# Scores of the middle attention: two products over 128 partitions in place of three over 64

## The chip, the core and the metric

The kernel runs on one core of a Trainium2 chip, as one launch. The metric is the device time of that core in microseconds (us). Engines are named as in the profile: PE is TensorE (matmuls, and transposes as matmuls), PEld its weight loads, DVE VectorE, ACT ScalarE, POOL GpSimd, SP SyncE.

## The reference

Two layers of a graph network over 625 nodes with 512 features. Each layer adds a graph part and a linear attention to x, and then a feed-forward part. What the change touches is the feed-forward part of the first layer, a full softmax attention whose weights a small router picks out of three sets:

```python
def gqa(x, wq, wk, wv, wo, n_kv):        # 8 heads of 64, x is the layer norm of 625 rows
    q = (x @ wq).reshape(B, S, N_HEADS, D_K).transpose(0, 2, 1, 3)
    k = (x @ wk).reshape(B, S, n_kv, D_K).transpose(0, 2, 1, 3)
    ...
    scores = jnp.einsum('bhqd,bhkd->bhqk', q, k) / jnp.sqrt(jnp.float32(D_K))
    attn = jax.nn.softmax(scores, axis=-1)
    out = jnp.einsum('bhqk,bhkd->bhqd', attn, v)
    out = out.transpose(0, 2, 1, 3).reshape(B, S, D_MODEL)
    return out @ wo
```

The second layer then has an edge part (20625 edges) and, as its feed-forward part, a product of the input with 128 matrices of 512x512, which takes the greater part of the kernel's time.

## The kernel before, in words

All engines run programs written out by hand, each in its own fixed order, and wait for each other by semaphores. The rows are tiled as 5 tiles of 125 nodes (T = 5, P = 125). Wide matmul operands are float32 values split in two: a rounded part ("h", written by ACT as it copies PSUM out) and the rest ("l", the value minus the rounded part, written by DVE). A product of two such operands is `product` (L1694 to L1700): h by h (L1698), h by l (L1699) and l by h (L1700), three matmuls into one PSUM group; l by l is left out.

PSUM is used as four slots of two banks. Work that fills a slot is a unit; `UNITS` lists all units in the order in which PE makes them, the slot is the unit's number modulo 4, and `begin` waits until the unit that had the slot last is drained.

The middle attention's units are, in order: `q1` (4 units: queries, transposed, two heads of 64 features on the 128 partitions of each), `k1` (4, keys likewise), `v1` (3, values by rows), then the list `ATTENTION`, then `proj1`.

- For each `q1` and `k1` unit PE runs 24 matmuls; ACT writes QFh or KFh (`upper`, L807) and DVE QFl or KFl (L1377). Between them ACT rounds the next weight matrix (L817), and POOL takes its rest (L687).
- An item is one tile of 125 queries of one head, 40 in all, five to a head. For an item PE makes `score` (two halves of 314 keys, each one `product` over the 64 partitions of the head's features); DVE takes the negated row maximum (negmax, L1388); ACT the exponential with its row sum (L967); DVE corrects the sum and inverts it (L1393, L1396); POOL scales the row (L732); PE turns it in five transposes (`probT`, L1920); ACT and DVE split the turned item (L978 and L807 for PTh, L1405 and L1124 for PTl).
- The order on PE is score of item i, then the transposes of item i-2. Once the five items of a head are turned, `attn` follows: 30 matmuls (PTh, PTl by VFh, VFl), whose result ACT and DVE split into XTh and XTl. Around it two items are taken together: score, score, attn, ten transposes.

The lines that matter are those of `score` on PE:

```python
u, r, o = ("score", item), item // T // 2, 64 * (item // T % 2)
begin(u)
if item == 0:
    wait_drained(pe, ("k1", K - 1))
...
ins = product(slot(u)[0:P, h, 0:HN], (QFh[o:o + 64, r, c], QFl[o:o + 64, r, c]),
              (KFh[o:o + 64, r, keys], KFl[o:o + 64, r, keys]), True, True)
```

Of the kernel before, what the change touches and what calls it, by code (L numbers as in the profile page):

```python
# [4 lines left out]
F32 = mybir.dt.float32  # L5
# [10 lines left out]
P = 125  # L16
T = N // P
K = D // 128
NT = 628
# [137 lines left out]
def splits(unit):  # L157

    return sum(u[0] in SPLIT for u in UNITS[:NUMBER[unit] + 1])
# [16 lines left out]
def halves(buf):  # L176

    return buf.rearrange("p (h n) -> p h n", h=2)


def build(nc, A, out):
    with ExitStack() as ctx:
        def sb(name, shape, dt, scope=ctx):
            return scope.enter_context(nc.sbuf_tensor(name, shape, dt))
# [3 lines left out]


        X = sb("X", [P, T, D], F32)  # L190
        XN = sb("XN", [P, T, D], F32)
        XTh = sb("XTh", [128, K, NT], F32R)
        XTl = sb("XTl", [128, K, NT], F32R)
# [100 lines left out]
            OTl = sb("OTl", [128, K, NT], F32R, s)  # L294

        with ExitStack() as s:
            QFh = sb("QFh", [128, K, NT], F32R, s)
            QFl = sb("QFl", [128, K, NT], F32R, s)
            KFh = sb("KFh", [128, K, NT], F32R, s)
            KFl = sb("KFl", [128, K, NT], F32R, s)  # L300
            VFh = sb("VFh", [P, T, D], F32R, s)
            VFl = sb("VFl", [P, T, D], F32R, s)
            PTh = sb("PTh", [P, T, NT], F32R, s)
            PTl = sb("PTl", [P, T, NT], F32R, s)
            prob = sb("prob", [P, 4, NT], F32, s)

        with ExitStack() as s:
            K2h = sb("K2h", [P, T, D], F32R, s)
# [165 lines left out]

        def slot(unit):
            return PS[:, 2 * SLOT[unit]:2 * SLOT[unit] + 2, :]

        def name_of(w):
            return WEIGHTS[w][0]
# [319 lines left out]
        def _(act):  # L799
# [6 lines left out]
            def upper(unit, dst, src, scale=1.0):  # L806
                a.activation(dst, src, ACT.Copy, scale=scale).then_inc(upper_ready, 1)  # L807

            def wait_filled(unit):
                act.wait_ge(filled, NUMBER[unit] + 1)  # L810
# [135 lines left out]
            transposed_upper("xt1")  # L946
            weight_upper(WEIGHT["F_q"])
            weight_upper(WEIGHT["F_k"])
            for stage, dst, scale in (("q1", QFh, DH ** -0.5), ("k1", KFh, 1.0)):
                for f in range(K):  # L950
                    u = (stage, f)
                    wait_filled(u)
                    upper(u, halves(dst[:, f]), slot(u)[:, :, 0:HN], scale)
                weight_upper(WEIGHT["F_v" if stage == "q1" else "F_o"])
            for m, tiles in enumerate(TILES):
                u = ("v1", m)
                wait_filled(u)
# [131 lines left out]
        def _(dve):  # L1089
# [280 lines left out]
            v.scalar_tensor_tensor(out=choice[0:1, 0:1], in0=choose[0:1, 1:2], scalar=2.0, in1=choose[0:1, 2:3],  # L1370
                                   op0=ALU.add, op1=ALU.mult).then_inc(chosen, 1)
            transposed_rest("xt1")
            for stage, up, dst, scale in (("q1", QFh, QFl, DH ** -0.5), ("k1", KFh, KFl, 1.0)):
                for f in range(K):
                    u = (stage, f)
                    dve.wait_ge(upper_ready, splits(u))
                    v.scalar_tensor_tensor(out=halves(dst[:, f]), in0=slot(u)[:, :, 0:HN], scalar=scale,  # L1377
                                           in1=halves(up[:, f]).bitcast(F32), op0=ALU.mult, op1=ALU.subtract).then_inc(drained_v, 1)
            for m, tiles in enumerate(TILES):
                u, j = ("v1", m), slice(tiles[0], tiles[-1] + 1)  # L1380
                rest(u, VFl[:, j], slot(u)[0:P, 0:len(tiles), :], VFh[:, j])
# [305 lines left out]
        def _(pe):  # L1687
# [201 lines left out]
            for part, n in ATTENTION:  # L1889
                if part == "score":  # L1890
                    item = n
                    u, r, o = ("score", item), item // T // 2, 64 * (item // T % 2)
                    begin(u)
                    if item == 0:
                        wait_drained(pe, ("k1", K - 1))
                    c = tile_columns(item % T)
                    for h in range(2):
                        keys = slice(h * HN, (h + 1) * HN)
                        ins = product(slot(u)[0:P, h, 0:HN], (QFh[o:o + 64, r, c], QFl[o:o + 64, r, c]),
                                      (KFh[o:o + 64, r, keys], KFl[o:o + 64, r, keys]), True, True)  # L1900
                    finish(ins)
                if part == "attn":
                    head = n
                    u, c = ("attn", head), slice(head // 2 * 128, head // 2 * 128 + 128)
                    begin(u)
                    wait_drained(pe, ("probT", T * head + T - 1))
                    for h in range(2):
                        queries = slice(h * HN, (h + 1) * HN)
                        for t in range(T):
                            ins = product(slot(u)[:, h, 0:HN], (VFh[:, t, c], VFl[:, t, c]), (PTh[:, t, queries], PTl[:, t, queries]),  # L1910
                                          t == 0, t == T - 1)
                    finish(ins)
                if part == "probT":
                    turned = n
                    u = ("probT", turned)
                    begin(u)
                    pe.wait_ge(prob_ready, turned + 1)
                    for t in range(T):
                        dst = slot(u)[0:P, t // 4, (t % 4) * P:(t % 4 + 1) * P]
                        ins = nc.tensor.transpose(dst, prob[:, turned % 4, tile_columns(t)], ident[0:P, 0:P])  # L1920
                    finish(ins)
# [209 lines left out]
```

## Time and profile before

| | us |
|---|---|
| median of three runs (lowest, highest) | 2633.79 (2628.89, 2633.82) |
| the profiled execution, its own time | 2621.18 |
| its span in the profile | 2619.2 |
| the middle attention, first score to last attn product | 413.8 to 553 |
| its items before the first attn (clock at half) | 420.6 to 438.7 |

The span is measured from the first recorded instruction to the last; 2.0 us of the execution's time lie around it. PE is busy for 94% of the span. The clock granted to PE is given as a share of 2.4 GHz: 1.00 is that, 0.50 is 1.2 GHz. The last slices of the page (from 1000 us on) are the product with 128 matrices, where PE is busy throughout; the middle attention lies in slices 7 to 9 of 40.

### The profile page before, as it was taken

Reading aid. Unit: us, or ns where it says so; the run is one execution under the profiler, and the core shown is the slowest. Engines: PE = TensorE matmul, PEld = TensorE weight load, DVE = VectorE, ACT = ScalarE, POOL = GpSimd, SP = SyncE. Lnnn points to the kernel's source line nnn. Section 1 sums busy time; section 2 is a strip of 40 time slices with the busy share of each in tenths; the row PEclk is TensorE's granted clock in tenths of the full one; section 3 lists DMA queues with packets and bytes.
Section 4 is the critical chain, followed back from the end, with each engine's and each line's share of the span. In section 5 each row is a group of like instructions: output and inputs, shape, how many; then the busy total and the mean of one; then the engine's idle time right before and its main releaser. Section 6 shows DMA issues by size and latency. Waiting matters only on the chain.

```text
span 2619.2 us, 34595 instructions
## 1 busy us (share of the span) xinstructions
PE 2457.5 (94%) x11680; PEld 2056.2 (79%) x11680; DVE 1802.2 (69%) x2675; ACT 924.4 (35%) x1128; POOL 1649.6 (63%) x724
## 2 busy tenths in 40 slices
PE   6989978976899679999999999999999999999999
PEld 6878877865799667777777777777777777777777
DVE  8974324547588657777777777777777777777775
ACT  3732224522389552223223232223222322322231
POOL 0024322228888745777777777777777777777773
PEclk9989877988799779999999999999999999999999
DMA  3024010011433200221212212122122221221211
GB/s 77 16 68 162 17 65 17 1 49 47 110 87 92 79 38 33 97 84 76 96 64 96 95 65 96 69 91 96 64 96 80 80 96 64 96 91 69 96 64 36
DMA packets 49889, 190.90 MB, mean 73 GB/s; under 512 B 13300, under 2 KB 17911, under 8 KB 33444
## 3 DMA queue, kind: packets, MB, share of 16 engines
q1 hardware_dynamic: 35728, 177.90, 19.4%
q0 software_dynamic: 13200, 10.75, 1.9%
q10 hardware_dynamic: 900, 1.44, 0.2%
q8 instruction: 37, 0.61, 0.1%
q14 instruction: 24, 0.20, 0.0%
HBM read 177.54 MB, written 12.35 MB: 72 GB/s over the span
## 4 chain that ended last, share of the span: by engine, by line
PE 79%; DVE 10%; POOL 6%; issue 2%; ACT 2%; DMA 1%; SPq 0%; DVEq 0%; ACTq 0%; POOLq 0%
PE PS L1698 25%; PE PS L1700 25%; PE PS L1699 25%; POOL gatW L751 3%; POOL XN L751 2%; PE PS L1776 2%; DVE hotS L1151 1%; POOL gat L751 1%; DVE hotD L1152 1%; DVE negmax L1388 1%; DVE PTl L1405 1%; PE PS L1962 1%; PE PS L1920 0%; PE PS L1963 0%; DVE XN L1115 0%
## 5 line engine op out<-in xcount | busy, mean ns | idle before, releaser
L1648 DVE SCALAR_TENSOR_TENSOR XN<-PS,attn,XN 125x512 f32<-125x512 f32 x1083 | 805.4, 749 | 439.9 <-PE PS L1700 431.4
L789 POOL TENSOR_TENSOR OPl<-TS,OPh 128x1024 fp32r<-128x1024 f32 x256 | 677.5, 2647 | 116.7 <-ACT OPh L1061 116.7
L789 POOL TENSOR_TENSOR OPl<-RAW,OPh 128x1024 fp32r<-128x1024 f32 x192 | 555.2, 2892 | 273.4 <-ACT OPh L1061 273.4
L1698 PE MATMUL PS<-OPh,XTh 128*125 128x512 f32 x1280 | 507.6, 397 | 2.0 <-DVE attn L1602 2.0
L1700 PE MATMUL PS<-OPh,XTl 128*125 128x512 f32 x1280 | 506.1, 395 | 0.0
L1699 PE MATMUL PS<-OPl,XTh 128*125 128x512 f32 x1280 | 503.7, 394 | 0.0
L1061 ACT ACTIVATE OPh<-TS 128x1024 fp32r<-128x1024 f32 x256 | 271.8, 1062 | 530.0 <-PE PS L1700 517.3
L1061 ACT ACTIVATE OPh<-RAW 128x1024 fp32r<-128x1024 f32 x192 | 203.8, 1062 | 579.1 <-PE PS L1700 579.1
L1698 PE MATMUL PS<-OPh,Sh 128*125 128x512 f32 x1024 | 404.3, 395 | 3.1 <-DVE XN L1645 3.1
L1700 PE MATMUL PS<-OPh,Sl 128*125 128x512 f32 x1024 | 403.4, 394 | 0.0
L1699 PE MATMUL PS<-OPl,Sh 128*125 128x512 f32 x1024 | 402.1, 393 | 0.0
L1699 PEld LDWEIGHTS PS<-OPl,XTh 128*125 128x125 f32 x1280 | 238.7, 187 | 60.4
L1700 PEld LDWEIGHTS PS<-OPh,XTl 128*125 128x125 f32 x1280 | 238.0, 186 | 61.2
L1698 PEld LDWEIGHTS PS<-OPh,XTh 128*125 128x125 f32 x1280 | 237.5, 186 | 60.1 <-DVE attn L1602 2.2
L687 POOL TENSOR_TENSOR Wl<-Wraw,Wh 128x2048 fp32r<-128x2048 f32 x15 | 69.2, 4615 | 255.0 <-ACT Wh L817 254.9
L1698 PEld LDWEIGHTS PS<-OPh,Sh 128*125 128x125 f32 x1024 | 189.5, 185 | 50.6 <-issue 3.9
L1962 PE MATMUL PS<-hotE,msgh 125*128 125x314 f32 x660 | 201.5, 321 | 28.8 <-DVE msgl L1506 21.6
L1700 PEld LDWEIGHTS PS<-OPh,Sl 128*125 128x125 f32 x1024 | 190.0, 186 | 48.1
L1699 PEld LDWEIGHTS PS<-OPl,Sh 128*125 128x125 f32 x1024 | 190.1, 186 | 47.7
L1963 PE MATMUL PS<-hotE,msgl 125*128 125x314 f32 x660 | 198.9, 316 | 0.0
L1962 PEld LDWEIGHTS PS<-hotE,msgh 125*128 125x128 f32 x660 | 130.2, 197 | 32.5 <-issue 29.1
L751 POOL DMA_INDIRECT gatW<-nodes,dstI x90 | 134.8, 1497 | 29.0 <-issue 27.1
(345 smaller groups left out, 3587.6 us busy)
## 6 DMA issues: line engine op xcount, KB each, us to landing
RAW<-in_values SPq DMA_DIRECT2D x64, 2048.0 KB, 7.5
filters<-filt SPq DMA_DIRECT2D x14, 672.0 KB
fil<-filters SPq DMA_DIRECT2D x11, 840.0 KB
Wraw<-in_ffn SPq DMA_DIRECT2D x4, 1024.0 KB, 5.3
Wraw<-in_L_q SPq DMA_DIRECT2D x2, 1024.0 KB, 5.1
Wraw<-in_L_k SPq DMA_DIRECT2D x2, 1024.0 KB, 8.7
Wraw<-in_L_v SPq DMA_DIRECT2D x2, 1024.0 KB, 7.3
gatW<-nodes,dstI POOLq DMA_INDIRECT x90
```

The source lines that it names most:

```text
L687: g.tensor_tensor(Wl[SIDE[w]][:], Wraw[SIDE[w]][:], Wh[SIDE[w]][:].bitcast(F32), ALU.subtract).then_inc(w_split, 1)
L751: g.indirect_dma_start(gats[c % RING][:, u, :], None, nodes, bass.IndirectOffsetOnAxis(ap=dstI[:, t:t + 1], axis=0)).then_inc(gathered[c % ...
L789: g.tensor_tensor(OPl[:, j], operand_source(j, parity), OPh[:, j].bitcast(F32), ALU.subtract).then_inc(op_lower, 1)
L1061: a.activation(OPh[:, j], operand_source(j, parity), ACT.Copy).then_inc(op_upper, 1)
L1151: v.tensor_scalar(hotS[:, parity, u, :], iota16[:, 0:N + 1], srcF[:, bass.ds(t, 1)], None, ALU.is_equal)
L1648: v.scalar_tensor_tensor(out=XN[:, t], in0=PS[0:P, bank, :], scalar=w, in1=XN[:, t], op0=ALU.mult, op1=ALU.add).then_inc(v_added, 1)
L1698: mm(dst, lh, rh, start=start, stop=False, skip_group_check=resumed)
L1699: mm(dst, lh, rl, start=False, stop=False, skip_group_check=resumed)
L1700: return mm(dst, ll, rh, start=False, stop=stop, skip_group_check=resumed)
L1776: ins = mm(PS[0:P, count_bank(n), 0:HALF], hotS[:, parity, u, s * P:(s + 1) * P], hotD[:, parity, u, 0:HALF], start=(c == m * COUNT_CHUNKS ...
L1962: mm(dst, msgh[:, q, u, c_], hot, start=(first and u == 0), stop=False)
L1963: ins = mm(dst, msgl[:, q, u, c_], hot, start=False, stop=(last and u == EB - 1))
```

## The change

The queries of a head now stand on 128 partitions, the rounded part on partitions 0 to 63 and the rest on 64 to 127 (`queries_both`). The rounded part of the head's keys stands on both halves (`keys_high`), and so does their rest (`keys_low_a` for heads 0 to 3, `keys_low_b` for heads 4 to 7). One matmul over 128 partitions with `keys_high` gives h by h and l by h together, one with the keys' rest gives h by l and l by l. An item has 4 score matmuls instead of 6, all over 128 partitions, and l by l is now part of the result.

To write these layouts ACT has 2 copies for a `q1` unit instead of 1 and 4 for a `k1` unit instead of 1, each of 64 partitions by 628; DVE has 2 and 4 instead of 1. Some of them write other partitions than they read. `keys_low_a` lies in the storage of XN, which holds the layer norm until the transposes `xt1` have read it and is written again after the attention.

```diff
@@ build: buffers @@
         X = sb("X", [P, T, D], F32)
+        with ExitStack() as s:
+            keys_low_a = sb("keys_low_a", [128, HEADS // 2, NT], F32R, s)
         XN = sb("XN", [P, T, D], F32)
...
-            QFh = sb("QFh", [128, K, NT], F32R, s)
-            QFl = sb("QFl", [128, K, NT], F32R, s)
-            KFh = sb("KFh", [128, K, NT], F32R, s)
-            KFl = sb("KFl", [128, K, NT], F32R, s)
+            queries_both = sb("queries_both", [128, HEADS, NT], F32R, s)
+            keys_high = sb("keys_high", [128, HEADS, NT], F32R, s)
...
             prob = sb("prob", [P, 4, NT], F32, s)
+            keys_low_b = sb("keys_low_b", [128, HEADS // 2, NT], F32R, s)
...
+        def keys_low(head):
+            return (keys_low_a if head < HEADS // 2 else keys_low_b)[:, head % (HEADS // 2)]
@@ ScalarE @@
-            for stage, dst, scale in (("q1", QFh, DH ** -0.5), ("k1", KFh, 1.0)):
-                for f in range(K):
-                    u = (stage, f)
-                    wait_filled(u)
-                    upper(u, halves(dst[:, f]), slot(u)[:, :, 0:HN], scale)
-                weight_upper(WEIGHT["F_v" if stage == "q1" else "F_o"])
+            for f in range(K):
+                u = ("q1", f)
+                wait_filled(u)
+                a.activation(halves(queries_both[0:64, 2 * f]), slot(u)[0:64, :, 0:HN], ACT.Copy, scale=DH ** -0.5)
+                upper(u, halves(queries_both[0:64, 2 * f + 1]), slot(u)[64:128, :, 0:HN], DH ** -0.5)
+            weight_upper(WEIGHT["F_v"])
+            for f in range(K):
+                u = ("k1", f)
+                wait_filled(u)
+                a.activation(halves(keys_high[0:64, 2 * f]), slot(u)[0:64, :, 0:HN], ACT.Copy)
+                a.activation(halves(keys_high[64:128, 2 * f]), slot(u)[0:64, :, 0:HN], ACT.Copy)
+                a.activation(halves(keys_high[0:64, 2 * f + 1]), slot(u)[64:128, :, 0:HN], ACT.Copy)
+                upper(u, halves(keys_high[64:128, 2 * f + 1]), slot(u)[64:128, :, 0:HN])
+            weight_upper(WEIGHT["F_o"])
@@ VectorE @@
-            for stage, up, dst, scale in (("q1", QFh, QFl, DH ** -0.5), ("k1", KFh, KFl, 1.0)):
-                for f in range(K):
-                    u = (stage, f)
-                    dve.wait_ge(upper_ready, splits(u))
-                    v.scalar_tensor_tensor(out=halves(dst[:, f]), in0=slot(u)[:, :, 0:HN], scalar=scale,
-                                           in1=halves(up[:, f]).bitcast(F32), op0=ALU.mult, op1=ALU.subtract).then_inc(drained_v, 1)
+            for f in range(K):
+                u = ("q1", f)
+                dve.wait_ge(upper_ready, splits(u))
+                for i in range(2):
+                    ins = v.scalar_tensor_tensor(out=halves(queries_both[64:128, 2 * f + i]), in0=slot(u)[64 * i:64 * i + 64, :, 0:HN],
+                                                 scalar=DH ** -0.5, in1=halves(queries_both[0:64, 2 * f + i]).bitcast(F32),
+                                                 op0=ALU.mult, op1=ALU.subtract)
+                ins.then_inc(drained_v, 1)
+            for f in range(K):
+                u = ("k1", f)
+                dve.wait_ge(upper_ready, splits(u))
+                for i in range(2):
+                    for o in (0, 64):
+                        ins = v.tensor_tensor(halves(keys_low(2 * f + i)[o:o + 64]), slot(u)[64 * i:64 * i + 64, :, 0:HN],
+                                              halves(keys_high[o:o + 64, 2 * f + i]).bitcast(F32), ALU.subtract)
+                ins.then_inc(drained_v, 1)
@@ TensorE, in the loop over ATTENTION @@
-                    u, r, o = ("score", item), item // T // 2, 64 * (item // T % 2)
+                    u, head = ("score", item), item // T
...
-                        ins = product(slot(u)[0:P, h, 0:HN], (QFh[o:o + 64, r, c], QFl[o:o + 64, r, c]),
-                                      (KFh[o:o + 64, r, keys], KFl[o:o + 64, r, keys]), True, True)
+                        mm(slot(u)[0:P, h, 0:HN], queries_both[:, head, c], keys_high[:, head, keys], start=True, stop=False)
+                        ins = mm(slot(u)[0:P, h, 0:HN], queries_both[:, head, c], keys_low(head)[:, keys], start=False, stop=True)
```

On PE, before. The rows stand where the second item after the first transposes is made: six score matmuls, five transposes (`ident`, `prob`), six score matmuls.

```order
L1698 MATMUL PS<-KFh,QFh 125x314
L1699 MATMUL PS<-KFl,QFh 125x314
L1700 MATMUL PS<-KFh,QFl 125x314
L1698 MATMUL PS<-KFh,QFh 125x314
L1699 MATMUL PS<-KFl,QFh 125x314
L1700 MATMUL PS<-KFh,QFl 125x314
L1920 MATMUL PS<-ident,prob 125x125 x5
L1698 MATMUL PS<-KFh,QFh 125x314
L1699 MATMUL PS<-KFl,QFh 125x314
L1700 MATMUL PS<-KFh,QFl 125x314
```

On PE, now, the same place.

```order
L1921 MATMUL PS<-keys_high,queries_both 125x314
L1922 MATMUL PS<-keys_low_a,queries_both 125x314
L1921 MATMUL PS<-keys_high,queries_both 125x314
L1922 MATMUL PS<-keys_low_a,queries_both 125x314
L1942 MATMUL PS<-ident,prob 125x125 x5
L1921 MATMUL PS<-keys_high,queries_both 125x314
L1922 MATMUL PS<-keys_low_a,queries_both 125x314
```

Each item has two matmuls fewer; the order of items, transposes and attn is the same.

On DVE, before, from the last operation of `xt1` to the first row maximum.

```order
L1136 CAST XTl<-XTl 128x4x3
L1377 SCALAR_TENSOR_TENSOR QFl<-PS,QFh 128x628 x4
L1377 SCALAR_TENSOR_TENSOR KFl<-PS,KFh 128x628 x4
L1124 TENSOR_TENSOR VFl<-PS,VFh 125x1024 x2
L1124 TENSOR_TENSOR VFl<-PS,VFh 125x512
```

On DVE, now.

```order
L1148 CAST XTl<-XTl 128x4x3
L1389 SCALAR_TENSOR_TENSOR queries_both<-PS,queries_both 64x628 x8
L1398 TENSOR_TENSOR keys_low_a<-PS,keys_high 64x628 x8
L1398 TENSOR_TENSOR keys_low_b<-PS,keys_high 64x628 x8
L1136 TENSOR_TENSOR VFl<-PS,VFh 125x1024 x2
L1136 TENSOR_TENSOR VFl<-PS,VFh 125x512
```

Eight operations have become twenty-four, at the same place ahead of those of `v1`.

## Rows read from the trace of the kernel before

**Rows 1.** Timeline, 423.7 to 430.5 us: start, length, instruction [idle before <-releaser].
```profile
427.09 0.81 DVE L1388 TENSOR_REDUCE negmax<-PS 125x1 f32<-125x628 f32 x1 [1.35 <-PE PS L1700]
```

**Rows 2.** Chain of waits, 420.5 to 440 us: start, length, what (us).
```profile
423.85 1.34 PE PS L1920 x5
425.19 0.55 PE PS L1698
425.75 0.26 PE PS L1699
...
427.05 1.34 PE PS L1920 x5
...
434.80 0.55 PE PS L1698
```

**Rows 3.** Timeline, 450.9 to 452.2 us.
```profile
451.16 0.31 PE L1699 MATMUL PS<-KFl,QFh 64*125 64x314 f32 x1
451.30 0.30 PE L1700 MATMUL PS<-KFh,QFl 64*125 64x314 f32 x1
...
452.08 0.81 DVE L1388 TENSOR_REDUCE negmax<-PS 125x1 f32<-125x628 f32 x1 [0.39 <-PE PS L1700]
```

**Rows 4.** Waits, 413 to 548 us: total, times, longest (us).
```profile
DVE negmax L1388 <- PE PS L1700: 12.2, 12, 3.2
```

**Rows 5.** Groups by shape, 413 to 548 us: busy us, mean ns, idle before.
```profile
L1124 DVE TENSOR_TENSOR XTl<-PS,XTh 64x628 fp32r<-64x628 f32 x7 | 5.7, 809 | 38.8 <-ACT XTh L807 38.8
L807 ACT ACTIVATE XTh<-PS 64x628 fp32r<-64x628 f32 x7 | 4.8, 688 | 29.2 <-PE PS L1700 29.2
```

**Rows 6.** Timeline, ACT and DVE alone, evacuation of keys and values.
```profile
387.95 0.70 ACT L807 ACTIVATE KFh<-PS 128x628 fp32r<-128x628 f32 x1 [0.98 <-PE PS L1700]
391.43 0.70 ACT L807 ACTIVATE KFh<-PS 128x628 fp32r<-128x628 f32 x1 [2.78 <-PE PS L1700]
...
398.99 1.91 ACT L817 ACTIVATE Wh<-Wraw 128x2048 fp32r<-128x2048 f32 x1
...
399.12 0.81 DVE L1377 SCALAR_TENSOR_TENSOR KFl<-PS,KFh 128x628 fp32r<-128x628 f32 x1 [2.67 <-ACT KFh L807]
405.01 1.23 DVE L1124 TENSOR_TENSOR VFl<-PS,VFh 125x1024 fp32r<-125x1024 f32 x1 [5.08 <-ACT VFh L807]
```

**Rows 7.** Timeline, start of the attention, 411.5 to 421.5 us.
```profile
413.77 0.40 PE L1698 MATMUL PS<-KFh,QFh 64*125 64x314 f32 x1 [1.46 <-DVE PTl L1383]
...
414.82 4.53 POOL L687 TENSOR_TENSOR Wl<-Wraw,Wh 128x2048 fp32r<-128x2048 f32 x1 [9.22 <-ACT Wh L817]
...
416.97 2.40 DVE L1393 SCALAR_TENSOR_TENSOR rowsum<-prob,rowsum 125x1 f32<-125x1 f32 x1 [0.35 <-ACT prob L967]
```

**Rows 8.** Stretches: length, busy PE PEld DVE ACT POOL, granted clock, DMA, GB/s.
```profile
420.60:438.70 18.10, 17.62 (x62) 14.88 (x62) 9.28 (x27) 8.29 (x22) 4.75 (x6) 0.50 0.00 0
...
482.10:485.40 3.30, 2.38 (x14) 1.90 (x14) 3.23 (x11) 2.40 (x6) 1.58 (x2) 1.00 0.02 5
485.40:488.80 3.40, 3.40 (x14) 3.40 (x15) 0.65 (x3) 0.88 (x2) 0.79 (x1) 0.51 0.00 0
570.80:574.20 3.40, 1.79 (x15) 1.54 (x16) 3.00 (x9) 1.57 (x4) 1.28 (x2) 1.00 0.77 219
```

**Rows 9.** Chain of waits, 355 to 580 us: attn products begin (PE), end (ACT).
```profile
438.69 0.60 PE PS L1698
...
445.89 0.70 ACT XTh L807
...
455.88 0.38 PE PS L1698
460.51 0.70 ACT XTh L807
...
485.25 0.43 PE PS L1698
...
491.40 0.70 ACT XTh L807
```

## The prediction

> **What bounds the kernel now.** I read the chain of waits through the middle attention first, then the timeline at its two clock levels, the granted clock by stretches, and last the evacuations ahead of it. Since the part after the attention starts from its result, what is saved on the chain here reaches the end of the kernel. The attention has two regimes.
>
> At half clock, before the first attn products, the chain is PE alone: five transposes of 1.34 us, a first score product of 0.55 and five more of 0.26 (0.55 + 5 x 0.26 = 1.85), so an item takes 1.34 + 1.85 = 3.20, the step from 423.85 to 427.05 [rows 2]. DVE waits for PE in each, as in the 1.35 us at 427.09 [rows 1]. Five scores stand so on the chain, from 421.99 to 434.80, at that step of 3.20.
>
> At full clock DVE is the chain. It has per item the row maximum, the two short operations of the sum, and the two subtractions of PTl. It waits for a score in one place per head: the first score behind the transposes that had to wait for POOL, with 0.39 us idle before the row maximum at 452.08 [rows 3]. The chain has the same piece in six heads (the scores at 450.98, 465.75, 480.37, 496.64, 511.26 and 527.56). The twelve waits of 12.2 us in all [rows 4] are these six (6 x 0.39 = 2.3), and those ahead of and in the first head (9.8). All other scores at full clock are made while DVE still works on the item before.
>
> **Two products fewer per item.** A product costs what its 314 columns cost: at half clock 0.26 [rows 2], at full clock 0.145 (0.14 to 0.15 from start to start) [rows 3]. A product over 128 partitions costs no more: a unit of keys is 24 of them, and the units follow each other by 3.48 us (387.95 to 391.43), which is 0.145 each [rows 6]. The removed products are the cheap ones, not the first with its 0.55.
> - Half clock: 5 scores x 2 x 0.26 = 2.6 us. PE stays the bound: an item becomes 3.20 - 0.52 = 2.68. DVE had 1.35 us idle per item there [rows 1] and keeps some 0.8.
> - Full clock: 2 x 0.145 = 0.29 per score, of which only the six on the chain count: 0.29 is under the 0.39 that DVE waits, so all of it counts: 6 x 0.29 = 1.7 us. Behind that point DVE is the bound again, up to the next attn.
> - The first three scores at 413.77 give nothing. They start when DVE is through with the padding of PTl, and the row sum behind them takes 2.40 us, until 419.37, and POOL's split of a weight ends at 419.35 [rows 7]; the change leaves both where they are.
>
> Sum of the products: 2.6 + 1.7 = 4.3 us.
>
> **The evacuations.** For queries ACT has 2 copies per unit in place of one, for keys 4. The nearest rows for 64 partitions by 628 are 0.69 us on ACT and 0.81 on DVE [rows 5], as long as for 128 partitions (0.70 and 0.81 [rows 6]). The trace shows none that reads one half of the partitions and writes the other; I bound that between these values and twice them, and take these values, since the partition count alone cost nothing. Keys: ACT 4 x 0.70 = 2.8, DVE 4 x 0.81 = 3.25, both under the 3.48 of PE for a unit. DVE starts when ACT's four are done, so a unit is free 6.1 us after it is filled instead of 1.5; its slot is wanted again four units, 13.9 us, later. The last unit of keys, filled at 398.4, is ready at about 404.6, and the first score wants it at 413.77. DVE's next work is the values at 405.01 [rows 6], 0.4 later, and behind it are 5 us idle. ACT's weight copy of 1.91 us moves from 398.99 to about 401.2, done at 403.1; ACT's next copy starts at 403.95, and POOL's split behind it, some 4.5 us as in [rows 7], ends near 408, and the projection that wants it comes after the last attn. The same goes for the queries. So this costs nothing, and what hides it is PE's own unit of 3.48 and then the values' 15 us. With twice the duration, keys would take DVE 6.5 us a unit: 26 us from 391 to 417, with the values' rests behind, and the first score would come some 6 us late. That is the upper end, +6; the lower end is 0, since nothing shortens.
>
> **The clock.** The attn products of a head take 4.63 us at full clock (455.88 to 460.51), and 6.15 where the clock fell as they began (485.25 to 491.40) [rows 9]. This happened in three of the six heads (485, 516, 533), 1.52 each. Ahead of the fall at 485.4 PE had done two scores over 64 partitions and had then waited for DVE; the clock came back after attn products over 125 [rows 8]. And from 420.6 to 438.7 PE was busy for 17.62 of 18.10 us with scores over 64 partitions and transposes, yet the clock stayed at half [rows 8], until attn products had run from 438.69 on. I read from this that products over half the partitions hold the clock less well than those over all of them. The scores now fill 128 partitions, with two thirds of the products, so 4 x 128 against 6 x 64 for an item. I take it that two of the three falls go: 2 x 1.52 = 3.0 us. Bounds: all three go, 4.6, or three more come, -4.6.
>
> **The sum.** 4.3 + 3.0 = 7.3 us, against the execution of the profile 2621.2 - 7.3 = 2613.9. The median of the runs is 2633.8, 12.6 above that execution; the same kernel spreads that much, with nothing in the trace to say where. Against the median it is 2626.5; I say 2626.
>
> **Rivals.**
> 1. Only the products count, the clock falls as before: 4.3 us, 2629.5. For it: where the clock falls is settled by where the scores lie when it is looked at, and that shifts anyway. Against it: rows 8.
> 2. The clock rises already among the first head's items, since their products fill the array. Then its attn takes 4.63 instead of 7.20 us (438.69 to 445.89 [rows 9]), 2.6 more, and some three items take 2.0 (a head's 14.4 less 4.63, over 5) instead of 2.68, 2.0 more: 7.3 + 4.6 = 11.9, 2621.9. Against it: the transposes are half of PE's time there, and under them it did not rise.
> 3. Slower: with fewer products PE is less busy, the clock falls in the middle of the items and stays at half through a whole head. A head at half clock costs 5 x 2.68 + 7.2 = 20.6 us. At full it costs 14.4: from 455.88 to 485.25 are two heads, 14.7 each [rows 9], less 0.29. That is 6.2 more. It decides from the first such head on, since 6.2 is over 4.3. With three such heads, and the 4.6 us of the present falls among them: 18.6 - 4.6 - 4.3 = 9.7 slower, 2643.5. For it: PE's busy share in the items at full clock does fall. Against it: DVE set the pace at full clock before as well, and the clock held through the items of every head at least up to its attn [rows 8, 9].
> 4. The evacuations across partitions cost twice the rows: 6 late, 7.3 gained: 2632.5.
>
> The Trainium skill speaks for rival 3. "TensorE: Matmul & The Clock Gate", Part 1, has the clock granted by how busy PE has been recently, and Part 4 says that transposes do not count as busy in the same way; by both, an item with two products fewer holds the clock worse, and the time would be rival 3's. This trace agrees only in part: from 570.8 to 574.2 PE ran nothing but transposes (1.79 us busy of 3.40), and the clock stayed at 1.00 [rows 8].
>
> **How the numbers follow.** Forecast 0.45, rival 1 0.27, rival 2 0.15, rival 3 0.07, rival 4 and the rest 0.06. The range for 8 in 10 reaches from rival 2 with the third fall gone as well and a run on the low side of the spread, 2616, to rival 4 with one on the high side, 2634. A difference of 0.2% (5.3 us) is about what a measurement of this kernel can tell from none. The forecast and rival 2 lie beyond it, rival 1 inside: faster 0.45 x 0.85 + 0.15 + 0.27 x 0.3 = 0.61, slower 0.08 (rival 3 and a little of the rest), the same 0.31.
>
> **What would show it.** In the profile after: items before the first attn 2.68 us apart instead of 3.20, if the clock is at half there; score products at 0.26 and 0.145 over 128 partitions; about 0.1 us of idle before the row maximum behind the waited transposes in place of 0.39; the first score at the same 413.8; the keys' last subtraction done near 404.6; attn products of 4.6 us in at least five of the six heads. I would be wrong if the clock falls ahead of attn as often as now (then 4.3 is all), if copies across partitions take longer than 0.87 us, or if the part after the attention gives the time back.

## The result: twice the gain that was forecast

| | before | after |
|---|---|---|
| median (lowest, highest), us | 2632.75 (2626.07, 2644.18) | 2617.89 (2604.74, 2625.02) |
| span of the profiled execution | 2619.2 | 2605.8 |
| first score | 413.77 | 417.27 |
| middle attention, first score to the start of the last head's XTh | 139.5 | 122.5 |
| of it at half clock | 44.4 | 10.2 |
| rest of the span behind it | 2066.0 | 2066.0 |

The ratio of the times is 0.9939 [0.9929, 0.995], from 20 runs of each: 14.9 us faster, where 7 were forecast. One execution in all, of a padded kernel below, took 3068.05 us at a mean clock of 0.735; its kernel's ratio leaves it out. In the two profiles the attention is 17.0 us shorter. It begins 3.5 us later, from work ahead of the changed part, as the first copy of queries out of PSUM shows, before and after:

```profile
374.03 0.70 ACT L807 ACTIVATE QFh<-PS 128x628 fp32r<-128x628 f32 x1 [7.98 <-PE PS L1700]
377.55 0.69 ACT L956 ACTIVATE queries_both<-PS 64x628 fp32r<-64x628 f32 x1 [7.78 <-PE PS L1722]
```

From there to the first score are 39.74 us before and 39.72 after. In three profiles of the change, of one and the same kernel, the first score stands at 417.27, 420.88 and 425.77 us. This is some of the spread that the prediction could not place; some lies behind the attention, where the rest of the span was 2063 to 2076 us in the twelve profiles, with no relation to the scores.

The stretches of the attention by granted clock come first (start and end, length, busy time of PE, PEld, DVE, ACT and POOL, clock, DMA share, GB/s), one for the kernel before and four for the kernel after:

```profile
417.20:444.50 27.30, 23.42 (x83) 20.70 (x84) 13.41 (x33) 9.96 (x26) 8.49 (x9) 0.50 0.00 1
...
420.70:424.10 3.40, 0.00 (x1) 0.03 (x1) 3.33 (x5) 0.81 (x3) 2.94 (x2) 1.00 0.00 0
424.10:427.50 3.40, 3.40 (x15) 3.40 (x16) 0.98 (x4) 1.44 (x5) 0.79 (x1) 0.50 0.00 0
427.50:529.90 102.40, 81.45 (x538) 71.89 (x537) 69.16 (x193) 61.17 (x155) 29.59 (x38) 1.00 0.00 1
529.90:536.70 6.80, 4.87 (x20) 4.35 (x19) 2.53 (x6) 1.51 (x4) 0.57 (x1) 0.50 0.01 2
```

Before, the clock was at half from 417.2 to 444.5 us, under the same kind of items [rows 8]. Now it falls at 424.1, where PE's wait for its first transposes ends, and is back after 3.40 us of scores and transposes; then it holds for 102 us, through the first head's attn products and six heads with theirs. The chain of waits shows what that does (start, length, what), after:

```profile
424.10 1.36 PE PS L1942 x5
425.46 0.26 PE PS L1921
425.72 0.26 PE PS L1922
425.98 0.26 PE PS L1921
426.24 0.28 PE PS L1922
426.54 0.81 DVE negmax L1410
427.35 0.08 DVE rowsum L1415
...
428.39 0.72 DVE negmax L1410
...
430.14 0.73 DVE negmax L1410
...
435.56 0.38 PE PS L1720
...
440.19 0.70 ACT XTh L811
...
449.65 0.38 PE PS L1720
...
454.28 0.70 ACT XTh L811
```

At 424.10 it looks like [rows 2], with four products in place of six. From 427 on DVE is the chain, at 1.75 us an item, where PE at half clock took 3.20. The attn products take 4.63 us already in the first head (435.56 to 440.19), against 7.20 [rows 9], and 4.63 to 4.65 in the six heads behind it.

The one place of a head where DVE waited for a score [rows 3] has two more rows before (transposes and first score product), and reads now, in the timeline after:

```profile
450.20 0.78 PE L1920 MATMUL PS<-ident,prob 125*125 125x125 f32 x5 [0.41 <-POOL prob L732]
450.91 0.40 PE L1698 MATMUL PS<-KFh,QFh 64*125 64x314 f32 x1
...
444.51 0.78 PE L1942 MATMUL PS<-ident,prob 125*125 125x125 f32 x5 [1.12 <-POOL prob L736]
445.05 0.39 PE L1921 MATMUL PS<-keys_high,queries_both 128*125 128x314 f32 x1
445.27 0.30 PE L1922 MATMUL PS<-keys_low_a,queries_both 128*125 128x314 f32 x1
...
445.92 0.80 DVE L1410 TENSOR_REDUCE negmax<-PS 125x1 f32<-125x628 f32 x1
```

The row maximum has no idle time ahead of it. The first score product starts 0.54 us after the transposes (444.51 to 445.05), where it was 0.71 before (450.20 to 450.91). The waits of DVE for a score (total, times, longest) fell from 12.2 us in 12 times [rows 4] to

```profile
DVE negmax L1410 <- PE PS L1922: 3.3, 2, 2.4
```

The evacuations of the last unit of keys, timeline after, ACT and then DVE:

```profile
401.89 0.69 ACT L962 ACTIVATE keys_high<-PS 64x628 fp32r<-64x628 f32 x1 [0.68 <-PE PS L1722]
402.59 0.69 ACT L963 ACTIVATE keys_high<-PS 64x628 fp32r<-64x628 f32 x1
403.29 0.69 ACT L964 ACTIVATE keys_high<-PS 64x628 fp32r<-64x628 f32 x1
404.00 0.69 ACT L811 ACTIVATE keys_high<-PS 64x628 fp32r<-64x628 f32 x1
...
404.72 3.28 DVE L1398 TENSOR_TENSOR keys_low_b<-PS,keys_high 64x628 fp32r<-64x628 f32 x4 [0.20 <-ACT keys_high L811]
408.50 1.22 DVE L1136 TENSOR_TENSOR VFl<-PS,VFh 125x1024 fp32r<-125x1024 f32 x1 [0.51 <-ACT VFh L811]
```

The two copies that write the other half of the partitions (L963, L964) take 0.69 us like the two that stay, four on DVE take 3.28 (3.25 forecast), and they end 0.5 us before DVE's next work.

### The profile page after: what moved, and what is told of

Its sections match the earlier page's. It is cut to its first block, busy times and chain, and to the rows that moved or that the text cites. A ratio compares the mean times of both kernels' runs of the same rounds, so it can differ in the third digit from the quotient of the medians.

```text
span 2605.8 us, 34467 instructions
## 1 busy us (share of the span) xinstructions
PE 2429.7 (93%) x11600; PEld 2030.4 (78%) x11600; DVE 1816.4 (70%) x2691; ACT 935.5 (36%) x1144; POOL 1651.3 (63%) x724
## 4 chain that ended last, share of the span: by engine, by line
PE 77%; DVE 10%; POOL 8%; issue 2%; ACT 2%; DMA 0%; SPq 0%; DVEq 0%; ACTq 0%; POOLq 0%
PE PS L1720 24%; PE PS L1722 24%; PE PS L1721 24%; POOL gatW L755 5%; POOL XN L755 2%; PE PS L1798 2%; DVE hotS L1163 1%; DVE hotD L1164 1%; POOL gat L755 1%; DVE PTl L1427 1%; DVE negmax L1410 1%; PE PS L1984 0%; DVE XN L1127 0%; PE PS L1985 0%; DVE XTl L1136 0%
```

## The experiments

Beside the copies, two things change at once: how many products a score half has, and over how many partitions. The theory: the partitions bring most of it, since scores over 128 raise the clock and hold it. The rival: the smaller number of products does. Each kernel's row gives its attention and its time at half clock in the profile, and the time against the runs of the kernel before beside it.

| scores | attention | at half clock | median | ratio to before |
|---|---|---|---|---|
| before: three over 64 | 139.5 | 44.4 | 2632.75 | |
| the change: two over 128 | 122.5 | 10.2 | 2617.89 | 0.9939 [0.9929, 0.995] |
| again | 123.8 | 13.7 | 2618.43 | 0.9949 [0.9923, 0.9975] |
| a third time | 123.6 | 13.7 | 2615.9 | 0.9942 [0.9921, 0.9964] |
| three over 128 (a discarded one added) | 125.5 | 10.2 | 2620.1 | 0.995 [0.9933, 0.9968] |
| three over 128 (zeros in the other head's half) | 125.6 | 10.2 | 2618.93 | 0.9947 [0.9927, 0.9967] |
| two over 64, old layout | 144.5 | 71.7 | 2644.84 | 1.0051 [1.0031, 1.0071] |
| two over 64, new layout | 148.4 | 85.3 | 2639.55 | 1.0028 [1.0007, 1.0049] |
| three over 64 and one over 128 | 158.6 | 47.8 | 2648.8 | 1.0062 [1.0038, 1.0087] |
| the change, one split later | 120.3 | 10.2 | 2610.52 | 0.9918 [0.9893, 0.9943] |
| again | 118.3 | 3.4 | 2612.94 | 0.9916 [0.9894, 0.9937] |
| before, the same split later | 137.0 | 41.0 | 2633.97 | 0.9996 [0.9977, 1.0015] |

The attention and its half clock are those of one profiled execution each. The repeats of the change have 15.7 and 15.9 us less than the kernel before in place of 17.0; the 1.1 to 1.3 between them lie where the clock was at half for longer, at the last attn and at the first transposes. The kernel with three over 128 and a discarded product and the change itself have the same falls, so their difference of 3.0 is clean of this. The mean clock of a whole execution, which every run has, says the same: its median is 0.952 to 0.956 in each of the seven measurements with scores over 128 partitions, 0.947 to 0.948 in those of the kernel before, and 0.940 in the two with two products over 64.

### Three products over 128 partitions

```diff
+mm(slot(u)[0:P, h, 0:HN], queries_both[:, head, c], keys_low(head)[:, keys], start=True, stop=True)
 mm(slot(u)[0:P, h, 0:HN], queries_both[:, head, c], keys_high[:, head, keys], start=True, stop=False)
```

The change with one more product per score half, whose result the next one overwrites.

> The changed kernel with a third score product per half of the keys, again over 128 partitions: queries_both by the keys' rest, whose result the next product overwrites. So an item has six score products as before the change, but over all partitions. If the gain is one of the partitions filled (the clock rises with the first items and does not fall ahead of attn, and a score starts sooner behind the transposes), nearly all of it stays: the first head's items at full clock, no fall in the six heads, the first score product 0.54 us behind the transposes' start at full clock instead of 0.71, attention 13 to 16 us shorter than before, time 11 to 15 us below the kernel before. If the gain is one of the number of products (my forecast's 4.3 us, and a PE that is less busy), it goes: time within 3 us of the kernel before.

2620.1 us: with as many products as before, 13 of the 15 us are there. Its stretches by clock:

```profile
421.90:425.30 3.40, 3.16 (x14) 3.19 (x15) 0.43 (x3) 1.57 (x4) 0.89 (x2) 0.50 0.00 0
425.30:531.10 105.80, 90.81 (x616) 83.00 (x614) 70.92 (x195) 61.27 (x155) 29.77 (x38) 1.00 0.00 1
```

It is the pattern of the change. The first head, from its first transposes to its XTh, takes 17.2 us, against 25.3 before and 16.1 after. Among the heads at full clock it tells the two parts of the waited score apart, by two neighbouring distances from one row maximum to the next: 2.23 + 1.80 before, 2.03 + 1.76 here, 1.75 + 1.76 after. So 0.24 us a head come from the partitions and 0.28 from the two products (0.29 forecast).

### Two products over 64 partitions, in the old layout

```diff
-ins = product(slot(u)[0:P, h, 0:HN], (QFh[o:o + 64, r, c], QFl[o:o + 64, r, c]),
-              (KFh[o:o + 64, r, keys], KFl[o:o + 64, r, keys]), True, True)
+mm(slot(u)[0:P, h, 0:HN], QFh[o:o + 64, r, c], KFh[o:o + 64, r, keys], start=True, stop=False)
+ins = mm(slot(u)[0:P, h, 0:HN], QFh[o:o + 64, r, c], KFl[o:o + 64, r, keys], start=False, stop=True)
```

The kernel before without the product of the queries' rest with the keys' rounded part.

> The kernel before with the third score product left out (queries' rest by keys' rounded part, so that the scores lack it): four products per item, all over 64 partitions. If the number of products counts, this has all that the change took away from PE: 12 to 16 us below the kernel before. If the partitions filled count, it has only the products: items 2.68 us apart at half clock in the first head (2.6 us saved), 0.29 us per head at full clock (1.7 us), the first score product still 1.34 us (half clock) and 0.71 us (full clock) behind the transposes' start, the clock falling ahead of attn in three heads or more; time 1 to 5 us below the kernel before, or as slow as it if the clock falls in more heads.

2644.84 us, 12 slower than before with a third of the score work gone, where 1 to 5 us less, or the same time, was expected. Three of its stretches:

```profile
423.30:443.60 20.30, 19.31 (x68) 16.58 (x69) 10.02 (x28) 9.08 (x24) 5.53 (x7) 0.50 0.00 1
453.80:460.60 6.80, 5.95 (x24) 5.57 (x23) 2.09 (x8) 1.75 (x4) 1.58 (x2) 0.50 0.01 1
467.50:477.70 10.20, 9.21 (x33) 8.31 (x34) 5.24 (x15) 4.45 (x12) 3.15 (x4) 0.50 0.01 2
```

In the first head the items follow each other by 2.68 us, to the hundredth what the prediction worked out for the change, and the head is 3.0 us shorter (22.3 against 25.3). Then the clock falls in five of the six heads behind, for 41 us in all, where before it fell for 3.4 us in three. This is the mechanism of rival 3 of the prediction, though in pieces of 3.4 to 10.2 us and not through whole heads: the attention is 5.0 us longer, where rival 3 had 9.7. The other 7 us of the time are not located; in this profile 7 lie behind the attention, as they do in a repeat of the change (2073 against 2066). The mechanism belongs to scores over 64 partitions.

### The same two products, in the new layout

```diff
-mm(slot(u)[0:P, h, 0:HN], queries_both[:, head, c], keys_high[:, head, keys], start=True, stop=False)
-ins = mm(slot(u)[0:P, h, 0:HN], queries_both[:, head, c], keys_low(head)[:, keys], start=False, stop=True)
+mm(slot(u)[0:P, h, 0:HN], queries_both[0:64, head, c], keys_high[0:64, head, keys], start=True, stop=False)
+ins = mm(slot(u)[0:P, h, 0:HN], queries_both[0:64, head, c], keys_low(head)[0:64, keys], start=False, stop=True)
```

The change with its evacuations, the scores over partitions 0 to 63 alone; the queries' rest is left out.

> The changed kernel's layouts and evacuations (24 subtractions on VectorE and 24 copies on ScalarE for queries and keys), but the two score products only over partitions 0 to 63, that is queries rounded by keys rounded and by keys' rest (queries' rest is left out). Against the kernel with two products over 64 partitions in the old layout it differs in the evacuations and in that all heads use partitions 0 to 63. If the evacuations are hidden, as I worked out, the two have the same time within 2 us, 1 to 5 us below the kernel before. If they cost (the change would then have gained more than its time shows), this one is 3 us or more slower than the other.

2639.55 us, ratio 1.0028 [1.0007, 1.0049], against 1.0051 [1.0031, 1.0071] for the old layout. Neither expectation holds as it stands: the two are 5.3 us apart, with the new layout ahead, and both are slower than the kernel before. The intervals overlap, so the times alone cannot say what the copies cost. The profiles can: from the first copy of queries to the first score are 39.74 us here and 39.72 in the old layout, and 39.72 to 39.74 in all twelve profiles, so the extra copies cost nothing. The first transposes come 6.80 us after the first score here, 6.82 in the old layout. Behind that the clock falls in all six heads (85.3 us at half in all), and the attention is 3.9 us longer than in the old layout.

### Three products over 128 partitions, half of them zeros

```diff
+a.activation(halves(keys_high[64:128, 2 * f]), slot(u)[64:128, :, 0:HN], ACT.Copy, scale=0.0)
+a.activation(halves(keys_high[0:64, 2 * f + 1]), slot(u)[0:64, :, 0:HN], ACT.Copy, scale=0.0)
...
+ins = product(slot(u)[0:P, h, 0:HN], (QFh[:, head // 2, c], QFl[:, head // 2, c]),
+              (keys_high[:, head, keys], keys_low(head)[:, keys]), True, True)
```

The queries lie as before, two heads on 128 partitions, and the keys of a head are zero in the other head's half. The useful work is exactly that of the kernel before.

> Three score products over 128 partitions, in which half of the partitions does no useful work: the queries stand as before, two heads on 128 partitions, and the keys of a head have zeros on the other head's partitions (both rounded part and rest). If it is the number of partitions that an instruction names which holds the clock and lets the score start sooner behind transposes, this acts like three products over 128 partitions with real numbers: 11 to 15 us below the kernel before. If it is how much of the array multiplies numbers other than zero, the clock acts as before the change (half clock in the first head, falls ahead of attn in about three), and only the sooner start remains: 0 to 4 us below the kernel before.

2618.93 us, 14 below the kernel before. Its stretch at full clock:

```profile
427.60:533.40 105.80, 90.81 (x614) 82.88 (x613) 71.05 (x196) 61.33 (x156) 30.06 (x38) 1.00 0.00 1
```

It stands beside the stretch of the kernel with the discarded product, with the same length and the same 90.81 us of PE. What counts is the number of partitions that the products name; that half of what they multiply by is zero changes nothing. This is also the plainest answer to where the gain comes from: the kernel before, with its operands padded to 128 partitions, has 14 of the 15 us.

### A useless product over 128 partitions beside the three over 64

```diff
+mm(slot(u)[0:P, h, 0:HN], QFh[:, r, c], KFh[:, r, keys], start=True, stop=True)
 ins = product(slot(u)[0:P, h, 0:HN], (QFh[o:o + 64, r, c], QFl[o:o + 64, r, c]),
```

> The kernel before with a fourth, useless product ahead of the three of each half of the keys, over all 128 partitions (queries' rounded part of two heads by keys' rounded part of two heads); the next product overwrites its result. PE has 8 score products per item instead of 6: two over 128 partitions, six over 64. If the clock is held by how much PE does over full partitions, it rises among the first head's items and falls ahead of attn in at most one head of six, and the time is below the kernel before in spite of the added work: 2 to 9 us, since items are then set by PE at 2.0 to 2.3 us. If added products only cost, the first head's items at half clock are 3.7 us apart, later ones 0.3 us more per item on the chain: 5 to 12 us slower than before.

2648.8 us, 15 slower than before: a miss for the expectation that one product in four over all partitions would bring the clock up, and beyond the 5 to 12 of its rival too. The items of the first head are 4.31 us apart where 3.7 were expected. Its stretches:

```profile
418.60:452.70 34.10, 34.10 (x104) 25.44 (x104) 12.64 (x34) 10.57 (x28) 8.52 (x9) 0.50 0.00 1
469.70:551.70 82.00, 81.52 (x464) 64.43 (x464) 48.26 (x126) 40.58 (x102) 18.53 (x24) 1.00 0.00 1
```

In the first, PE is busy for all of 34.10 us, and the clock stays at half to the middle of the first head's attn. So the first head can stay at half clock without any idle time of PE in the records, whose ends are modelled. In the six heads behind, the clock fell twice (466.3 and 551.7) for 3.4 us each, against three times before.

The timeline of PE in this kernel shows a second thing:

```profile
473.46 0.39 PE L1899 MATMUL PS<-KFh,QFh 128*125 128x314 f32 x1
473.78 0.41 PE L1698 MATMUL PS<-KFh,QFh 64*125 64x314 f32 x1
474.03 0.30 PE L1699 MATMUL PS<-KFl,QFh 64*125 64x314 f32 x1
474.18 0.31 PE L1700 MATMUL PS<-KFh,QFl 64*125 64x314 f32 x1
474.41 0.41 PE L1899 MATMUL PS<-KFh,QFh 128*125 128x314 f32 x1
```

Four products take 0.95 us from start to start (473.46 to 474.41) where four at 0.145 are 0.58. From 128 partitions to 64 and back costs 0.37 us here, a cost that the expectation did not have. In the change, with transposes over 125 partitions and scores over 128, the step to the scores is shorter (0.54 us against 0.71).

### The change, with the split of one weight later

The prediction found 2.40 us lost in a row sum that ends with POOL's split of a weight [rows 7], and the change leaves that. Here ACT's rounding and POOL's split of L1_q, which only `proj1` wants, are moved behind the first items.

```diff
@@ POOL @@
-            split_weight(WEIGHT["L1_q"])
             for i in range(ITEMS):
...
+                if i == T + LAG:
+                    split_weight(WEIGHT["L1_q"])
@@ ACT @@
-            weight_upper(WEIGHT["L1_q"])
             for part, n in ATTENTION:
+                if (part, n) == ("attn", 0):
+                    weight_upper(WEIGHT["L1_q"])
```

> The changed kernel with the rounding (ScalarE) and the split (GpSimd) of the weight L1_q moved from the start of the attention into the pause ahead of the first head's evacuation. The row sum of the first item took 2.40 us there, until GpSimd's split ended, and the first exponential waited behind ScalarE's rounding. If the split is what holds it, the row sum takes 0.3 us or less, the first transposes start 2.5 to 3.5 us sooner after the first score (3.5 to 4.3 us instead of 6.83), and the time is 2 to 4 us below the changed kernel. If the row sum is slow for another reason (its first use), the start stays within 0.7 us and the time within 1 us of the changed kernel. The clock could also take part: with a shorter pause it may not fall at all, 1 us more.

> The changed kernel once more, as the reference on this chip for the runs beside it: 13 to 18 us below the kernel before, attention 122 to 123 us long, half clock only around the first transposes and at the last attn.

The first measurement gave 2610.52 us, 8 below the change on the same chip. The timeline of it at the start:

```profile
426.21 0.41 PE L1923 MATMUL PS<-keys_high,queries_both 128*125 128x314 f32 x1 [1.46 <-DVE PTl L1407]
...
428.85 0.16 DVE L1417 SCALAR_TENSOR_TENSOR rowsum<-prob,rowsum 125x1 f32<-125x1 f32 x1 [0.22 <-ACT prob L981]
...
430.25 0.78 PE L1944 MATMUL PS<-ident,prob 125*125 125x125 f32 x5 [2.04 <-POOL prob L735]
```

The row sum takes 0.16 us where it took 2.40, the first transposes come 4.04 us after the first score (before and after the change: 6.84 and 6.83), and the transposes take 0.78, full clock, so the clock did not fall. That is worth 3.5 us of attention against the repeat of the change on the same chip (123.8, where 122 to 123 was expected), and 2 to 4 us of time were expected, not 8, so it was measured again beside a third run of the change.

> The change, unaltered, beside the two late splits on one chip. It should repeat 0.994 to 0.995 of before, with the half clock of 3.4 us as the first transposes begin and the attention at 122 to 124 us.

> The change with L1_q's rounding and split put behind the first items, again, to measure how much it gives beside the change itself. Theory (the wait of 2.8 us between first score and first transposes goes, and with it the fall of the clock at the first items): the attention takes 120.3 us again against 122.5 to 123.8, so 3 us, and the ratio lies 0.001 below the change's. Rival (the first look's 8 us below the change was real): 0.9918, that is 0.003 below it, and then something outside the attention gives the rest.

The attention takes 118.3 against 123.6; 2.8 us of that lie between first score and first transposes (4.03 against 6.83), 1.7 in the first head, and the rest at the last attn, where the clock was at half for 3.4 us instead of 6.8. The times are 2612.94 and 2615.9, 3 us apart, ratios 0.9916 [0.9894, 0.9937] and 0.9942 [0.9921, 0.9964]. Two comparisons, of 8 and of 3 us, point the same way and the profiles show where, but each pair of intervals overlaps, so that the size stays open. These are the lowest medians here. The third run of the change missed one thing that was expected of it: its half clock at the first transposes lasted 6.8 us, not 3.4.

The split also shows at its new place, in the timeline of the first late-split kernel:

```profile
444.03 4.57 POOL L691 TENSOR_TENSOR Wl<-Wraw,Wh 128x2048 fp32r<-128x2048 f32 x1 [1.65 <-ACT Wh L822]
...
446.75 0.66 DVE L1429 TENSOR_TENSOR PTl<-PS,PTh 125x500 fp32r<-125x500 f32 x1
...
447.52 0.79 DVE L1412 TENSOR_REDUCE negmax<-PS 125x1 f32<-125x628 f32 x1
448.24 0.37 DVE L1417 SCALAR_TENSOR_TENSOR rowsum<-prob,rowsum 125x1 f32<-125x1 f32 x1
```

The row sum that starts under it ends with it again (448.61 against 448.60, 0.37 us for 0.15), while a subtraction and a row maximum that read PSUM take their usual 0.66 and 0.79 us under it. So the split holds up the row sum and not all of DVE.

### The kernel before, with the same split later

> The kernel before (three products over 64 partitions) with the same late rounding and split of L1_q. Theory A (the clock in the first head is a matter of the partitions that scores name): the first transposes come 4.0 instead of 6.8 us after the first score, 2.8 us are gained, but the clock falls among the first items as before and stays at half to the first attn, items 3.2 us apart; attention 136 to 137 instead of 139.5. Theory B (the pause of PE ahead of the first transposes is what drops the clock, and the change only got it back sooner): without the pause the clock holds here too, the items follow by 1.8 to 2.2 us, and the first head saves some 8 us, attention 131 or less.

2633.97 us against 2633.87 of the kernel before, ratio 0.9996 [0.9977, 1.0015]. The attention takes 137.0, as theory A had it: 2.5 us are gained in the profile, which a measurement of the whole cannot tell from none. The first head's stretch by clock, and under it the one behind:

```profile
426.90:450.80 23.90, 22.05 (x79) 19.07 (x78) 11.57 (x34) 12.33 (x29) 7.14 (x9) 0.50 0.00 1
450.80:478.10 27.30, 24.51 (x157) 21.37 (x156) 18.61 (x50) 15.76 (x40) 10.89 (x10) 1.00 0.00 1
```

PE's pause ahead of its transposes was 1.4 us here instead of 4.0, and the clock fell all the same, with the last of the scores over 64 partitions that PE had made since 424.23, and stayed down. With scores over 128 and a pause of 2.0 us it held, in two profiles. So the pause does not explain the low clock of the first head over 64 partitions. Over 128 the short fall goes with the pause: it is there in five profiles with 4.0 to 4.8 us of pause, and in neither with 2.0.

## Why the prediction was right, and too small

The forecast was 2626 us with a range of 2616 to 2634; it came out at 2617.9, in the direction given and near the lower end. The time is that of rival 2 and 4 us beyond. It lies in the range because the range reached to rival 2, not because the forecast's own sum held. By the steps of the prediction:

| step | forecast | measured |
|---|---|---|
| first head, first transposes to XTh | 2.6 | 9.2 |
| waited score in six heads | 6 x 0.29 = 1.7 | 6 x 0.52 = 3.1 |
| falls of the clock at attn | two of three, 3.0 | three of three, 4.6 |
| last head and start | 0 | 0.1 |
| evacuations | 0 | 0 |
| sum | 7.3 | 17.0 |

**The step that failed** is "PE stays the bound: an item becomes 3.20 - 0.52 = 2.68", with the argument against rival 2, "the transposes are half of PE's time there, and under them it did not rise". The clock rose after 3.4 us of these items, with the transposes still in them, and behind that DVE set the pace, at 1.75 an item. I had put the low clock of the first head down partly to the transposes, though the prediction's own reading said that products over half the partitions hold the clock less well. Taken seriously, that reading made rival 2 the forecast. The kernel with three products over 128 shows it: 8.1 of the 9.2 us of the first head come without any product being saved. Padding the old kernel with zeros gives the same.

**An item at half clock was mis-sized** beside that. The 2.68 was borne out for two products over 64. Over 128 the one item that began and ended at half clock took 2.20: from 424.10 to the next transposes at 426.30. The prediction held the first product's 0.55 for fixed; over 128 it is 0.26 (at 425.46), and the transposes behind the scores start sooner too. The 0.48 between 2.68 and 2.20 is the price of stepping from transposes over 125 partitions to scores over 64 and back. The same term is missing in the waited score at full clock: 0.24 us a head by the kernel with three over 128, 6 x 0.24 = 1.4 us, which is the whole of the miss in that row. The 0.39 us of idle time that I took for a cap was no cap: the distance between the two row maxima there shrank by 0.48, since without a wait a DVE instruction starts 0.08 before the record of the one ahead of it ends (445.92 against 445.72 + 0.28), and the next distance shrank by 0.04.

**The falls of the clock** were reasoned from the right cause and sized with caution. All three went, and in the six heads the clock did not fall in any of the seven profiles of kernels with scores over 128 partitions. A sum of 4.3 for the count and 3.0 for the clock had the weights wrong: of the 17.0 us of attention, 14.0 come from the partitions (three over 64 to three over 128) and 3.0 from the count. Without the partitions the count would have cost 5.0 (three over 64 to two over 64). That 3.0 comes near the 4.3 of the forecast is luck in part: the 2.6 us for the first head assumed half clock throughout, and 1.1 came of it under the higher clock. These runs do not separate whether the products over 64 themselves keep the clock low or the steps to them and back, which also cost PE time: every kernel with scores over 64 has both.

**Rival 3** came true where the change doesn't go: with two products over 64 the clock was at half for 71.7 us of the attention instead of 44.4, and the kernel was slower. With 128 partitions the count had no such effect: 10.2 us at half with three products and with two. The Trainium skill, "TensorE: Matmul & The Clock Gate", Part 1 ("What's actually happening"), says that the clock is set by how busy PE has been recently. The two products over 64 agree with it. The kernel with the useless product does not, if busy means that PE is running something: it ran for 34.10 of 34.10 us at 0.50, and the change for 3.40 of 3.40 and then had 1.00. No run here measures how much a product over 64 counts. The stretch of transposes at 1.00 that the prediction set against this (570.8 to 574.2) is weak evidence: PE ran nothing but transposes until 577.6 and was busy for only 2.8 of the 6.8 us, and at 577.6 the clock fell.

**The evacuations** were right, in the durations to 0.03 us: 0.69 and 0.82 us a copy whichever half is written, 3.28 on DVE within PE's 3.48 a unit, the last done at 408.0 (404.6 forecast, and the attention as a whole is 3.5 later), DVE's next work 0.5 us behind. One reading beside them was off and cost nothing: the 5 us of idle time lay ahead of the values' subtraction at 405.01; behind it were 4.4. A product over 128 partitions took what one over 64 did, 0.145 and 0.26. The Trainium skill, "TensorE: Matmul & The Clock Gate", "Why this matters for your kernels", says of a single product over 32 partitions that it takes the same time as one over 128; the trace agrees for 64.

The first score at "the same 413.8" was wrong by 3.5 us, from work that the change doesn't touch (from the first copy of queries on, the two kernels differ by 0.02).

## What to carry to other kernels

In this kernel a matmul over half the partitions took as much time as one over all of them (0.145 us at full clock), and beside transposes or products over more partitions it cost more, twice: in the step from one to the other, and in the clock of everything around it. Before counting products, look at how many partitions they name and at the granted clock of their stretch; padding with zeros was worth 14 us here without saving one product. And a product that is taken away can make a kernel slower, where the rest no longer holds the clock: over 64 partitions the removal of one in three made it 12 us slower.

## What the runs showed of the hardware

- **The granted clock follows the partitions named, not the data.** Scores over 64 kept it at 0.50 for 23.9 to 34.1 us in the first head (five kernels); scores over 128, zeros or not, had it back after 3.4 us in four profiles, after 6.8 in one, and in the two with the shorter pause it never fell there. Whether the products or the steps around them do it is open.
- **Changing the partition count costs time on PE.** At full clock the first score product starts 0.71 us after the transposes' start over 64, 0.54 over 128. At half clock an item with four products takes 2.68 over 64 and 2.20 over 128.
- **A short DVE instruction waited for a long POOL one.** The row sum over 125x1 took 2.40 us while POOL's split of 128x2048 ran, and ended with it; without the split beside it, 0.16. DVE instructions that read PSUM under the same split kept their usual time.
